# Macaron block on Trainium2: expert loops that open with paired experts' batch-0 rows while batch 1 is still routed

## The reference

```python
x = x + 0.5 * moe(layernorm(x))
x = x + lightning_attention(layernorm(x))
x = x + 0.5 * moe(layernorm(x))
# moe(x2d): 32 experts (256 -> 96 -> 256), 16 chunks (256 -> 128 -> 256)
sel = top_k(sigmoid(x2d @ gate_w.T), 4)         # w: softmax over the four
cw_large[token, sel] += w
cw_small[token, sel // 2] += w
a = silu(x2d @ Wg[e]) * (x2d @ Wu[e]) * cw[:, e]
out = sum(a_large @ Wd[e]) + 0.05 * sum(a_small @ cWd[e // 2])
```

## Time and profile before

| what | value |
|---|---|
| median of 3 runs | 561.28 us (561.24 to 561.94) |
| span of the profiled execution (its own time isn't among the three) | 560.4 us |
| PE busy | 523.7 us, 93% |
| DVE, ACT, POOL busy | 60%, 29%, 50% |
| PE's share of the chain that ended last | 75% |
| layer 0: start to tile 2's up product | 0 to 46.0 us |
| layer 0: expert loop after that | to about 144 us |
| attention, from there to its last output product | to 402.25 us |
| layer 1: to the end of tile 2's up product | to 439.1 us |

### The profile page before, as it was taken

One profiled execution on the slowest core, in us unless ns is written; L12 is line 12 of the kernel. 1 busy time (PEld: TensorE's weight loads), 2 busy tenths in 40 slices (PEclk: granted clock), 3 DMA queues, 4 the chain that ended last, 5 costly groups with the idle time before them and its releaser, 6 DMA issues.

```text
span 560.4 us, 10737 instructions
## 1 busy us (share of the span) xinstructions
PE 523.7 (93%) x3624; PEld 460.5 (82%) x3624; DVE 334.1 (60%) x940; ACT 162.6 (29%) x439; POOL 282.0 (50%) x301
## 2 busy tenths in 40 slices
PE   8789999999699999899999999999878899999977
PEld 7778888787568989799989988889867788788756
DVE  6854444444247989887667868677685444444432
ACT  4202222222234333434343333333220222222210
POOL 0045666663344766667555645455104566666420
PEclk9879999999889999999999999999997999999999
DMA  7989999777361331212121222221296522776637
GB/s 216 323 234 320 345 363 308 243 225 242 134 227 49 102 104 54 65 57 86 50 75 55 83 60 70 64 58 47 70 362 215 178 92 95 256 260 226 215 121 297
DMA packets 55233, 93.09 MB, mean 166 GB/s; under 512 B 7424, under 2 KB 37888, under 8 KB 55168
## 3 DMA queue, kind: packets, MB, share of 16 engines
q1 hardware_dynamic: 45952, 71.29, 39.2%
q0 software_dynamic: 6912, 18.88, 10.0%
q10 hardware_dynamic: 2304, 2.10, 1.1%
HBM read 79.67 MB, written 12.58 MB: 165 GB/s over the span
## 4 chain that ended last, share of the span: by engine, by line
PE 75%; DVE 9%; DMA 7%; issue 6%; POOL 2%; ACT 1%; SPq 0%; POOLq 0%; DVEq 0%
PE bank L1255 10%; PE bank L1357 9%; PE bank L1250 8%; PE bank L1411 7%; PE bank L1274 5%; PE bank L1276 5%; PE bank L1393 5%; PE bank L1368 4%; PE bank L1399 3%; PE bank L1379 3%; PE bank L1222 3%; PE bank L1139 2%; DMA decay_all<-xn_dram,ids 2%; PE bank L1125 2%; DMA shared<-z_dram 2%
## 5 line engine op out<-in xcount | busy, mean ns | idle before, releaser
L517 POOL DMA_INDIRECT decay_all<-xn_dram,ids x72 | 69.6, 966 | 109.9 <-PE bank L1222 40.2
L526 POOL DMA_INDIRECT z_dram<-probs_all,dest x72 | 70.2, 975 | 39.4 <-ACT probs_all L726 21.7
L962 DVE COPY wkv_sb<-bank 96x128 f32<-96x128 f32 x72 | 20.6, 287 | 93.1 <-PE bank L1265 93.1
L587 POOL TENSOR_TENSOR shared<-shared 128x512 f32<-128x512 f32 x39 | 50.2, 1286 | 42.9 <-DVE shared L1033 42.9
L718 ACT ACTIVATE rot<-bank 128x224 f32<-128x224 f32 x72 | 25.7, 357 | 140.8 <-PE bank L1255 140.8
L1255 PE MATMUL bank<-w_ch_sb,oT_all 128*128 128x256 f32 x256 | 65.7, 379 | 0.0
L1357 PE MATMUL bank<-split_sb 128*128 128x512 f32 x240 | 64.4, 404 | 0.3 <-POOL split_sb L559 0.3
L1411 PE MATMUL bank<-split_sb 128*128 128x256 f32 x384 | 53.5, 288 | 2.5 <-DVE split_sb L1056 2.3
L1250 PE MATMUL bank<-w_exp_sb,oT_all 128*128 128x192 f32 x256 | 52.6, 328 | 2.3 <-issue 1.2
L1411 PEld LDWEIGHTS bank<-split_sb 128*128 128x128 f32 x384 | 47.8, 190 | 3.2 <-issue 1.7
L1255 PEld LDWEIGHTS bank<-w_ch_sb,oT_all 128*128 128x128 f32 x256 | 46.9, 190 | 3.3
(11 more groups left out here) (167 smaller groups left out, 1032.7 us busy)
## 6 DMA issues: line engine op xcount, KB each, us to landing
shared<-w_up_piece SPq DMA_DIRECT2D x32, 448.0 KB, 5.3
w_exp_sb<-w_exp SPq DMA_DIRECT2D x32, 384.0 KB, 8.0
shared<-w_down_piece SPq DMA_DIRECT2D x32, 256.0 KB, 4.5
w_ch_sb<-w_ch SPq DMA_DIRECT2D x16, 384.0 KB, 5.9
shared<-z_dram SPq DMA_DIRECT2D x8, 512.0 KB, 6.1
wq_all<-wq SPq DMA_DIRECT2D x32, 128.0 KB, 2.1
decay_all<-decay SPq DMA_DIRECT2D x32, 128.0 KB, 2.2
wo_all<-wo SPq DMA_DIRECT2D x32, 128.0 KB, 2.1
```

What stands on the lines that cost most here:

```text
L517: pool.indirect_dma_start(out=xg[s], out_offset=None, in_=xn_dram[l][:, :], in_offset=bass.IndirectOffsetOnAxis(ap=ids[:, SEQ[t]:SEQ[t] + ...
L526: pool.indirect_dma_start(out=z_dram[l][:, :], out_offset=bass.IndirectOffsetOnAxis(ap=dest[:, SEQ[t]:SEQ[t] + 1], axis=0), in_=y_sb[s], i ...
L587: nc.gpsimd.tensor_tensor(dst, rope_a[r % 2], rope_b[r % 2], ALU.add).then_inc(roped, 1)
```

## The change

1. **Paired tiles.** Experts 0 to 19 no longer have a tile of 128 rows each. A tile of experts 2c and 2c+1 holds 64 rows of each, from batch 0 (t = 0 to 9, chunk c in common), and a later one (odd slots, in t = 24 to 35) the rest, from batch 1 with what batch 0 left over. The experts' own products run in two groups of 64 columns, the chunk's in the full 128. Experts 20 to 31 keep a whole tile. There are still 36 tiles, with quads at the same places.
2. **Batch 0 routed first.** In layer 0 only batch 0 is routed ahead of the loop, by half-width operations (`first_route`). In layer 1 all of batch 0's routing is done inside attention's units 18 to 30, logits by pairs of tiles, and the first two tiles are gathered there.
3. **Batch 1 routed inside the loop.** Its transposes and logits stand between up(1) and the step of t=2 (`second_turns`), its ranks at t=4, id products at t=8; DVE's pieces (`second_route`) stand between the products of t = 2 to 9. Tile 10's gather waits for the second ids. ACT copies turned rows and hidden rows of these tiles in DVE's place.
4. **Order of a step.** `rows_T(t + 1)` comes ahead of `down(t - 3)`; `down` multiplies by the chunk first, `up` by the expert first, so that the parts in half groups adjoin.
5. **Smaller parts.** The reload of `w_exp` in layer 1 is split (two chunks at unit 16, three after the last projection, eleven after attention), with a wait per chunk; the softmax weights are made at the end of the loop; a small table of places is loaded.

```diff
+PAIRED = 20
+PAIRS = PAIRED // 2
+HALF_ROWS = P // 2
+SEQ = [2 * c for c in range(PAIRS)] + list(range(PAIRED, E)) + [2 * c + 1 for c in range(PAIRS)]
+for q, at in enumerate((16, 22, 28, 33)):
+    SEQ.insert(at, E + q)
...
+                if t in (0, PAIRS):
+                    pool.wait_ge(xn_stored[l][t // PAIRS], 16 * SB)
+                    pool.wait_ge(ids_ready, 2 * l + 1 + t // PAIRS)
...
+            def own_groups(t):
+                q = SEQ[t]
+                if q < PAIRED:
+                    return [(slice(h * HALF_ROWS, (h + 1) * HALF_ROWS), up_rows(q // 2 * 2 + h), down_rows(q // 2 * 2 + h)) for h in range(2)]
...
-                for rows, _, _, down_e, down_c in row_groups(t):
-                    nc.tensor.matmul(y_ps[s][rows, 0:D], actT[s][0:MI, 0, rows], down_e, start=True, stop=False)
-                for rows, _, _, down_e, down_c in row_groups(t):
-                    ins = nc.tensor.matmul(y_ps[s][rows, 0:D], actT[s][:, 1, rows], down_c, start=False, stop=True)
+                for rows, _, down_c in chunk_groups(t):
+                    nc.tensor.matmul(y_ps[s][rows, 0:D], actT[s][:, 1, rows], down_c, start=True, stop=False, skip_group_check=True)
+                for rows, _, down_e in own_groups(t):
+                    ins = nc.tensor.matmul(y_ps[s][rows, 0:D], actT[s][0:MI, 0, rows], down_e, start=False, stop=True, skip_group_check=True)
...
-            tiles(0, MIN_TILES)
+            if l == 0:
+                rows_T(pe, 0, 0)
+            else:
+                rows_T(pe, 1, 1)
+            up(0)
+            if l == 0:
+                rows_T(pe, 0, 1)
+            up(1)
+            rows_T(pe, l, 2)
+            second_turns()
+            for t in range(2, MIN_TILES):
+                if t == 4:
+                    ranks(pe, l, 1)
+                if t == 8:
+                    id_matmuls(pe, l, 1)
+                    grain_row()
+                act_T(t - 2)
+                if t + 1 < MIN_TILES:
+                    rows_T(pe, l, t + 1)
+                if t >= 3:
+                    down(t - 3)
+                up(t)
...
+            rows_copied(act_e, l, 0)
+            rows_copied(act_e, l, 1)
+            if l == 1:
+                for i in range(SB, TT):
+                    residual_out(act_e, i)
+                second_roots()
+            silu(0)
+            rows_copied(act_e, l, 2)
+            silu(1)
+            second_turned()
```

More of the change, by code:

```diff
@@ L213, in macaron_kernel, with while_attending, chosen @@
[L213 to L217, removed]
+        HOT_Q, HOT_R = QW * SB // 2, P * SB // 2
+        def while_attending(l, p):
+            return l == 1 and p == 0
+        def chosen(l, p):
+            room = probs_all[:, S:2 * S] if while_attending(l, p) else shared[:, 0:S]
+            return room.rearrange("p (t k e) -> p t k e", t=SB, k=TOP_K)
@@ L673, in transposed @@
             if s == 1:
-                ins = nc.scalar.activation(xnT_hi[:, :, i * P:(i + 1) * P], rows, ACT.Copy)
+                ins = nc.scalar.activation(xnT_hi[i // SB][:, :, i % SB * P:(i % SB + 1) * P], rows, ACT.Copy)
             ins.then_inc(xnT_copied, 1)
@@ L726, in results_out, with second_roots, second_turned @@
                 nc.scalar.activation(y_sb[y], y_ps[s][:, 0:D], ACT.Copy).then_inc(y_copied, 1)
-            def tiles(a, b):
-                for t in range(a, b):
-                    silu(t)
-                    if t >= 2:
-                        results_out(t - 2)
+            def second_roots():
+                for i in range(SB, TT):
+                    root(act_e, 2 * l, i)
+            def second_turned():
+                for i in range(SB, TT):
+                    transposed(act_e, 2 * l, i, second_xT_ps[i - SB], i // 2 * 2 + 2)
             def alone(t):
@@ L850, in scaled_rows @@
             if s == 1 and i == 0:
-                dve.wait_ge(xn_stored[0], 16 * TT)
+                for p in range(2):
+                    dve.wait_ge(xn_stored[0][p], 16 * SB)
             if s >= 1:
@@ new lines, in first_route @@
+        def first_route(dve, tick, link):
+            dve.wait_ge(const_in, 16 * N_CONST)
+            link(nc.vector.tensor_copy(tok16[:], tok1))
+            for i in range(SB):
+                top_values(dve, 0, i, i + 1)
+                if i >= 1:
+                    top_index(dve, 0, i - 1)
+            top_index(dve, 0, SB - 1)
+            members(dve, link, 0, 0)
+            places_of(dve, link, 0, 0)
+            picked_slots(dve, link, 0, 0)
+            for k in range(TOP_K):
+                one_hots(dve, tick, 0, 0, k)
+            ids_of(dve, link, 0, 0)
@@ L1177, in logits, with ranks @@
             ins.then_inc(logits_mm, 1)
-        def moe_pe(pe, l):
-            first = l * SB
-            if l == 1:
-                keep_busy(14, bank[0])
-            for i in range(first, TT):
-                turn(pe, 2 * l, i)
-                if i > first:
-                    logits(pe, l, i - 1)
-            logits(pe, l, TT - 1)
-            keep_busy(10, bank[0])
-            pe.wait_ge(member_ready, l + 1)
+        def ranks(pe, l, p):
+            pe.wait_ge(member_ready, 2 * l + p + 1)
@@ new lines, in first_route_pe, with rows_T @@
+        def first_route_pe(pe):
+            for i in range(SB):
+                turn(pe, 0, i)
+                if i >= 1:
+                    logits(pe, 0, i - 1, i)
+            logits(pe, 0, SB - 1, SB)
+            keep_busy(6, bank[0])
+            ranks(pe, 0, 0)
+            keep_busy(14)
+            id_matmuls(pe, 0, 0)
+            keep_busy(13)
+        def rows_T(pe, l, t):
+            g, gn = slot_of(l, t, XG)
+            s, n = slot_of(l, t)
+            pe.wait_ge(xg_ready[l][t % XG], (t // XG + 1) * 16)
+            pe.wait_ge(xgT_ready[s], n)
+            for k in range(KD):
+                ins = nc.tensor.transpose(xgT_ps[s][:, k * P:(k + 1) * P], xg[g][:, k * P:(k + 1) * P], ident_sb[:])
+            ins.then_inc(xg_used[g], 1)
```

597 lines of the change are left out of this document (356 added, 241 removed).

## The result

| kernel | median (lowest to highest) | ratio to before, 95% interval |
|---|---|---|
| before | 561.38 us (561.24 to 561.94, 4 runs) | |
| changed | 570.74 us (568.39 to 572.75, 4 runs) | 1.017 (1.0141 to 1.0199) |
| changed, unaltered, in a later comparison | 570.09 us (567.41 to 572.70, 6 runs) | 1.0139 (1.0107 to 1.0172) |

What follows compares the result with a forecast made beforehand. TensorE, busy 93% of the span, was taken as the bound except at the two layer starts. Terms summed to +0.65 us, plus 7.2 for the clock: +7.85, 569.1 us, range 555 to 577.

Steps and rivals of the forecast that it cites:

- layer 1's start: Layer 1, last output product to tile 2's up product: batch 0 routed inside attention saves 23.4 us.
- Changes of the column split: Both expert loops: 43 more switches between full width and half groups per layer at 0.14 us, 6.0 us a layer.
- Tile 10's stall in layer 0: Layer 0's loop: TensorE waits 4.4 us for tile 10's rows, which need the second ids; bounds 1.3 to 5.1.
- I cost them at nothing: POOL's queue behind tile 10's gather: tile 11's gather and the scatters of tiles 3 and on add no time.
- The clock: Half clock after both layers' turns and tile 10's wait in layer 0: 2.4 us each, +7.2 in all.
- Layer 0's start: Up to tile 2's up product: routing half the tokens first gains 1.2 us, the turn taking most of the earlier gather.
- Attention: Attention between the layers: paired logits save about 3.5 us, added routing costs 5.0; net +1.5, from -1 to +4.
- free changes: Rival, paired-tile steps: switching between full and half width costs nothing, 557.1 us; chance 0.18.
- serial halves: Rival, paired tiles: the two halves run one after the other, 43 us more, 612 us; chance 0.03.
- a late start: Rival, layer starts: first ids still come at 34 us or attention doesn't hide routing, 577 us or more; chance 0.03.
- The clock that stays up: Rival: no half clock in the two turns or after tile 10's wait, 561.9 us; chance 0.12.
- Costlier turns: Rival, both layers' turns: ACT's queue makes a norm late by 3 us in each layer, 575 us; chance 0.15.

Runs made afterwards that it cites:

- again: The changed kernel, unaltered, profiled a second time in a later comparison; 570.09 us, 1.0139 of the kernel before.
- run 3: Changed kernel with resultless TensorE products in layer 0's two waits, 14 more at the first gather and seven in the turn; 568.43 us, 1.0117 of before.
- run 5: Changed kernel with the second half of batch 0's places in attention moved to the next unit; 571.98 us, 1.0191 of before.
- runs 1 and 2: Kernel before with experts 0 to 19's own products in two 64-column groups: halves apart (1) 593.7 us, 1.056; halves adjoining (2) 580.8 us, 1.0343.
- 4: Changed kernel with the softmax weights moved from behind the loop into t = 12 to 18; 573.05 us, 1.0182 of before.
- run 6: Changed kernel's layer 1 and attention with layer 0 as in the kernel before; 559.78 us, 0.9968 of before.
- 7 to 10: Run 6 with split places and seven idle products in layer 1's turn: 0.993 (10 repeats: 0.9933); 8 issues gathers first, 0.9881; 9 stages the first quad later, 0.9904.

## Why the prediction was right, and where not

**The sign and the size came out right, with errors that partly cancel.** The sum of the terms without the clock was +0.65; the loops gave +22.4 (again: +23.2) where +23.75 stood, layer 1's start -25.3 (again: -22.0) where -23.4 and a fall of +2.4 stood, attention +4.8 where +1.5 stood. The two largest terms, the changes of the column split in the loops and the time won at layer 1's start, were right as mechanisms.

**Changes of the column split: right, a little small.** 0.14 was taken from the seams of a quad, 0.173 measured: 43 changes come to 7.4 us a layer, not 6.0. That halves are not quarters was a fair doubt, and the difference is a fifth.

**Tile 10's stall in layer 0: mis-sized**, 4.4 forecast, 1.0 measured. Three sizes of that step were off. The sixteen id products and the grain row took 1.10 us (65.06 to 66.16) and not 1.95: eight with the last one's tail are no measure for sixteen. The gather was issued 2.9 us after the step's start (67.94), not 3.8. And it landed calmly: I carried the 5.0 to 6.5 us of 56 to 66 us forward, but the last weight chunk was issued at 63.24 and the staging only began at 73.62. So it came out near the lower bound of 1.3, and a little under it. In layer 1, where a calm landing was forecast, 1.35 stood and 1.03 came. The small terms were a little large as well: the ranks took 0.28 us (51.50 to 51.78) and not 0.55, the wait at t=5 0.39 and not 0.5. Timeline of SP:

```profile
63.24 0.43 SPq L470 DMA_DIRECT2D w_down_sb<-w_down  x1
73.62 2.52 SPq L435 DMA_DIRECT2D shared<-w_up_piece  x4
```

**"I cost them at nothing" was wrong for what stands behind that gather.** I named tile 11's gather, the scatters and SP's staging of the first quad, and priced each alone. Set free by the same event (the second tables), they meet: 2.8 MB of staging run at the moment when the late gathers have the least slack. In layer 1 this costs 0.7 us in one profile and 1.2 in the other, in layer 0 next to nothing.

**The clock: three falls of 2.4 were forecast; the places were partly others.** After tile 10 there is none in any profile; its wait was 1.0 us and not 4.4. Layer 0's start has two instead of one, because PE was also idle before the first tile (3.29 us, at 31.95), a stretch that I had taken to be no longer than in the kernel before; they cost 3.8 (run 3). Layer 1's turn has none in the first profile, and up(2) comes 11.4 us after the last output product, not 13.5: ACT's copies of batch 1 were there after 7.3 us and not 9.2. In the second it has one, granted 0.5 from 428.0 to 434.8, and up(2) comes at 14.7. So a fall costs 3.3 there. The tail's +1.8 and +0.8 go with falls too (546.7 to 553.6 in the first profile; run 5 has none there and a tail of 22.9). The sum, some 5.6 in the first profile and 8 in the second, is near 7.2 by luck of places. Nor do all low stretches of the kernel before lie on routing, as the prediction has it: one, from 148.7 to 159.0 (granted 0.50), lies on the weighted sums behind layer 0's loop. The changed kernel has only 3.4 us of low clock there in the first profile and 6.8 in the second, and gains next to nothing by it (17.4 us from the loop's end to the end of the sums before, 17.4 and 17.2 after), since PE stands still longer ahead of them (7.2 and 5.4 us, 4.6 before).

**Layer 0's start: right without the clock.** The gather was issued at 25.10 (25.9 forecast) and its rows were there 6.85 us later (5.3 forecast), two misses that nearly cancel. The transposes came at 31.95 (31.2 forecast) and, with PE kept busy, up(2) ended at 44.13 (44.8): a gain of 1.9 where 1.2 stood. That the turn eats most of the early gather holds: PE waits for ACT's copies at 40.0 in run 3, 40.6 forecast.

**Attention: mis-sized,** +1.5 (-1 to +4) forecast, +4.8 measured. From the end of one unit's output products to the next, in the first profile, against the kernel before: units 1 to 20 +1.2 us, units 21 to 25 and 27 -3.3, unit 26 +4.7, units 28 to 31 +2.1. Pairing the logits was priced rightly: PE's four waits for them, 4.4 us, lay in units 21, 23, 25 and 27, and one of 0.9 is left; those units give back 3.3, where 3.5 stood. Units 28 to 31, with the one-hots and the id products, take 2.1, where 1.75 stood for the id products; the picks (0.35 forecast) lie in unit 27. Two terms failed. The places, 2.9 forecast, cost 4.7: they were priced as DVE work, but they stand ahead of the unit's `split_output` on DVE, so PE's output products wait 3.17 us for it and then lose 1.2 at half clock; three of the small operations were stretched from 0.2 us to 1.16, 0.54 and 0.65. And units 1 to 20, where nothing was forecast, take 1.2 more, most of it in units 3 and 5, where PE waits for DVE by 0.34 us (at 211.64) and 0.87 us (at 230.96) as it did not before; why stays open.

**The rivals:** free changes (runs 1 and 2), serial halves (the same) and a late start are out. The clock that stays up is out for layer 0's start, and for layer 1's turn it held in the first profile alone: of the six profiles that run the new layer 1 without idle work in its turn (the changed kernel's two, runs 3 to 6) the other five show a fall there. Costlier turns were right for layer 0's, by the clock and not by ACT's queue.

## What to carry to other kernels

An early start that brings work in halves is paid in every step of the loop: count the changes of the column split along the new order, at 0.17 us each, before counting the wait that goes; here layer 0 lost 11 us in its loop for a start that gave 2 at best, with PE kept busy (run 3). Where one event sets several queues free, ask what each of them sends in that moment and which transfer has the least slack then. Work put into a gap of one engine must fit the order of that engine's queue: look at what stands behind it and who waits for that.

## What the runs showed of the hardware that was not expected

Three small DVE operations each ended 0.04 us after a POOL operation that ran beside them: L976 at 382.28 (POOL's at 382.24), L978 at 382.96 (382.92), L979 at 383.65 (383.61), by the rows of experiment 5. Alone, L976 takes 0.19 us (at 14.7 us), L978 and L979 0.18 (at 15.1 and 15.3). The second profile of the changed kernel shows the same three durations. The Trainium skill, SBUF — State Buffer, Who interferes with whom, says that a VectorE instruction with two SBUF inputs contends with a GpSimd instruction that reads SBUF, and that VectorE in a two-port mode, which `copy`, `cast` and `tensor_scalar` can enter, contends with GpSimd: whoever issues first gets the port pair that they share, and the other is blocked. These rows agree: the POOL operation began first each time, by 0.17, 0.23 and 0.12 us, and 0.19 us became 1.16; that L978 and L979 ran in a two-port mode no row shows.

The clock's falls are not fixed to the program: in layer 1's turn one profile of the same kernel has none and the other one of 6.8 us, and runs 3, 4 and 5, which leave that turn as it is, have 6.8 us each (run 6 has 3.4). With seven products put in, all four profiles (7 to 10) show none there.

A gather that lands in 2.7 us took 7.4 when it was issued 1.0 us behind the start of 2.8 MB of transfers from another queue.
